# Edge-network messages summed as two float32r parts against a one-hot stationary operand

## The reference, cut to what matters

```python
def _L1_gnn_ref(x, edge_index, edge_attr, W1, b1, W2, b2, W3, b3, W4, b4):
    row, col = (edge_index[0], edge_index[1])
    h = jnp.concatenate([x[row], edge_attr], axis=1)
    h = jax.nn.relu(h @ W1 + b1)                 # [edges, 128]
    h = h @ W2 + b2
    agg = scatter_mean(h, col, x.shape[0])       # sum over a node's edges / their count
    g = jnp.concatenate([x, agg], axis=1)
    g = jax.nn.relu(g @ W3 + b3)
    return g @ W4 + b4
...
x = _layernorm(x + _L1_gnn_ref(x, edge_index, edge_attr_32, ...), axis=-1)
```

## Time and profile before

| | us |
|---|---|
| median of 3 runs | 1945.89 |
| lowest and highest run | 1943.58, 1948.28 |
| span of the profiled execution, first to last instruction | 1945.2 |
| mean granted TensorE clock, as a share of full speed | 0.815 |
| busy over the whole span: PE, DVE, ACT, POOL | 1270.0, 998.1, 739.7, 578.6 |
| busy share: PE, DVE, ACT, POOL | 65%, 51%, 38%, 30% |

### The profile page before, as it was taken

The page is one execution under the profiler, slowest core; times in us unless marked ns, Lnnn a source line. Parts: engine busy times, 40 slices in busy tenths (PEclk is TensorE's granted clock), DMA queues, the critical chain, the costliest instruction groups (busy, mean ns, idle before and its releaser), DMA issues.

```text
span 1945.2 us, 47461 instructions
## 1 busy us (share of the span) xinstructions
PE 1270.0 (65%) x19829; PEld 1164.5 (60%) x19830; DVE 998.1 (51%) x2349; ACT 739.7 (38%) x2012; POOL 578.6 (30%) x683
## 2 busy tenths in 40 slices
PE   5201001000002787778998999998799998998897
PEld 3200000000001666667897999998799998898897
DVE  8000002000010666674457566565788888887887
ACT  5000000000001777773213344343566666655464
POOL 2777777777772000000001444441010010000000
PEclk8555555555555999889997999998899999899999
DMA  7431000001010999997474888884766661344442
GB/s 222 141 133 35 15 15 13 14 27 38 13 54 35 357 370 379 387 369 265 174 289 175 315 308 304 301 306 170 252 247 233 224 247 56 143 168 158 175 178 92
DMA packets 86126, 359.64 MB, mean 185 GB/s; under 512 B 23740, under 2 KB 35281, under 8 KB 78929
## 3 DMA queue, kind: packets, MB, share of 16 engines
q1 hardware_dynamic: 72594, 348.83, 48.3%
q0 software_dynamic: 13312, 7.69, 1.7%
HBM read 250.77 MB, written 105.68 MB: 183 GB/s over the span
## 4 chain that ended last, share of the span: by engine, by line
PE 45%; another core or an unknown queue 21%; issue 12%; DVE 12%; ACT 7%; DMA 2%; SPq 1%; POOL 0%; ACTq 0%; DVEq 0%; POOLq 0%
PE ps L2998 8%; PE ps L3619 7%; PE ps L2650 7%; PE ps L2986 6%; PE ps L3266 5%; PE ps L3633 2%; DMA arena<-recs 2%; PE ps L2525 2%; PE ps L2510 1%; DVE arena L3208 1%; DVE arena L3209 1%; ACT arena L2570 1%; DVE arena L2389 1%; PE ps L3322 1%
## 5 line engine op out<-in xcount | busy, mean ns | idle before, releaser
L2178 POOL DMA_INDIRECT recs<-arena x416 | 423.8, 1019 | 164.9 <-issue 132.2
L3056 POOL CAST arena<-arena 128x512 f32<-128x512 bf16 (+1 forms) x175 | 119.4, 684 | 615.2 <-DMA arena<-hot_out 447.8
L3619 PE MATMUL ps<-arena 125*128 125x64 bf16 x5850 | 192.8, 194 | 10.0 <-issue 10.0
L3619 PEld LDWEIGHTS ps<-arena 125*128 125x128 bf16 x5850 | 187.7, 99 | 11.9 <-issue 11.8
L2998 PE MATMUL ps<-arena 128*128 128x125 f32 x1300 | 182.2, 282 | 0.0
L3665 ACT ACTIVATE arena<-ps,arena 128x64 f32<-128x64 f32 x650 | 141.0, 333 | 102.9 <-PE ps L3633 102.9
L2510 PE MATMUL ps<-arena 128*128 128x128 bf16 x625 | 66.9, 232 | 166.5 <-issue 157.3
L3142 DVE TENSOR_TENSOR arena<-ps,arena 128x512 f32<-128x512 f32 (+1 forms) x175 | 114.1, 653 | 118.4 <-PE ps L2986 115.4
L3089 ACT ACTIVATE arena<-arena 128x512 f32<-128x512 f32 (+1 forms) x175 | 105.0, 601 | 171.4 <-DVE arena L3142 171.4
L2570 ACT ACTIVATE arena<-ps 128x512 f32<-128x512 f32 (+1 forms) x192 | 83.8, 523 | 215.8 <-remote 183.7
L2998 PEld LDWEIGHTS ps<-arena 128*128 128x128 f32 x1300 | 158.8, 192 | 0.0
(11 more groups left out here) (385 smaller groups left out, 2414.5 us busy)
## 6 DMA issues: line engine op xcount, KB each, us to landing
arena<-ids_out SPq DMA_DIRECT2D x100, 832.0 KB, 6.2
arena<-hot_out SPq DMA_DIRECT2D x75, 832.0 KB, 6.2
arena<-e_out SPq DMA_DIRECT2D x25, 1664.0 KB, 6.9
arena<-adj_out SPq DMA_DIRECT2D x41, 800.0 KB, 6.5
e_out<-arena SPq DMA_DIRECT2D x25, 1024.0 KB
hot_out<-arena SPq DMA_DIRECT2D x25, 832.0 KB, 7.1
adj_out<-arena SPq DMA_DIRECT2D x25, 800.0 KB, 6.4
e_out<-arena SPq DMA_DIRECT2D x25, 640.0 KB
```

Of the source, the lines that this page charges most:

```text
L2178: nc.gpsimd.indirect_dma_start(out=recs, out_offset=bass.IndirectOffsetOnAxis(ap=slot_row[:, t:t + 1], axis=0), in_=rec_in[:, t, :], in_of ...
L3056: nc.gpsimd.tensor_copy(hot_e[s % NH][:, 0:len(js), :], hot_in[d % 2][:, js[0]:js[0] + len(js), :])\
L3619: ins = M(bank(step % 4, C, k * C), hot_r[d % 2][r][0:NP_, j * SLOTS:(j + 1) * SLOTS], px3[:, block_of(d, j), piece, r * C:(r + 1) * C], s ...
```

## The change

The scatter's operands change places, and its data become float32r, a 32-bit type with a shorter mantissa to which the writing engine rounds. A message is split in two parts, the rounded value and what rounding left off, and both are summed.

- ACT makes relu twice from the same `pre`: first into the first half of `act_two` (rounded to float32r), then into `whole` (float32).
- POOL subtracts the first part from `whole` and writes the second part, rounded again, into the second half of `act_two`. It does this for step s behind the cast of step s + 1. Its cast now writes float32r, into a ring `hot_e` of four instead of eight.
- PE scatters with the one-hot (128 slots x 128 columns) as stationary operand and both parts, 256 columns, as the moving one. A block's bank holds nodes on the partitions and 2 x 128 columns. It waits for POOL's subtraction (`act_rest`) too.
- After the block's last scatter DVE adds the two halves (`tensor_reduce` to `both`), PE transposes the 125x128 result into the same bank behind the 256 columns, one step later, and DVE multiplies by the reciprocals one step after that. `hid_step` and all that hangs on it stand two steps (`TURN_SUM`) later.
- `pre` is a ring of three instead of two; `whole` and `both` lie in `y1`. The memsets of `sel` move from step G7 - 1 to G7 + 4.
- What is float32r lies in a buffer of its own, `rounded`, at the place in `arena` where `act_out` and `hot_e` were.

```diff
+NE = 4
...
-        act_out = [e1_at([128, 4 * HID]) for _ in range(4)]
...
-        hot_e = [e1_at([128, 4, 128]) for _ in range(NH)]
+        act_two = [rounded[:, k * 8 * HID:(k + 1) * 8 * HID].rearrange("p (k t h) -> p k t h", t=2, h=HID)
+                   for k in range(4)]
+        hot_e = [rounded[:, (32 + 4 * k) * HID:(36 + 4 * k) * HID].rearrange("p (k n) -> p k n", n=128)
+                 for k in range(NE)]
...
+        pre.append(e2_at([128, 4 * HID]))
+        whole = [y1[:, (13 + 4 * k) * HID:(17 + 4 * k) * HID] for k in range(2)]
+        both = [y1[0:NP_, (11 + k) * HID:(12 + k) * HID] for k in range(2)]
...
+        TURN_SUM = 2
...
-            return 7 * (tiles(c)[-1] + 1) + LAG + 2
+            return 7 * (tiles(c)[-1] + 1) + LAG + TURN_SUM + 2
...
                     pe.wait_ge(sem("act_relued"), s + 1)
+                    pe.wait_ge(sem("act_rest"), s + 1)
                     for k, j in enumerate(groups(d)[g]):
-                        ins = M(bank(4 + d % 2, NP_), act_out[s % 4][:, k * HID:(k + 1) * HID],
-                                hot_e[s % NH][:, k, 0:NP_], start=j == 0, stop=j == NT, skip_group_check=True)
+                        ins = M(bank(4 + d % 2, 2 * HID), hot_e[s % NE][:, k, :],
+                                act_two[s % 4][:, k, :, :].rearrange("p t h -> p (t h)"), start=j == 0, stop=j == NT,
+                                skip_group_check=True)
                     ins.then_inc(sem("act_summed"), 1)
+                d, at = divmod(step - LAG - TURN_SUM, 7)
+                if at == 0 and 1 <= d <= NT:
+                    d -= 1
+                    pe.wait_ge(sem("both_added"), d + 1)
+                    nc.tensor.transpose(bank(4 + d % 2, NP_, 2 * HID), both[d % 2], ident[0:NP_, 0:NP_])\
+                        .then_inc(sem("sum_turned"), 1)
...
         def pool_edge2(pool):
+            def rest(s):
+                n = len(groups(s // 7)[s % 7])
+                pool.wait_ge(sem("act_relued"), s + 1)
+                nc.gpsimd.tensor_tensor(act_two[s % 4][:, 0:n, 1, :],
+                                        whole[s % 2][:, 0:n * HID].rearrange("p (k h) -> p k h", h=HID),
+                                        act_two[s % 4][:, 0:n, 0, :].bitcast(F32), ALU.subtract)\
+                    .then_inc(sem("act_rest"), 1)
...
-                if s >= NH:
-                    pool.wait_ge(sem("act_summed"), s - NH + 1)
-                nc.gpsimd.tensor_copy(hot_e[s % NH][:, 0:len(js), :], hot_in[d % 2][:, js[0]:js[0] + len(js), :])\
+                if s >= NE:
+                    pool.wait_ge(sem("act_summed"), s - NE + 1)
+                nc.gpsimd.tensor_copy(hot_e[s % NE][:, 0:len(js), :], hot_in[d % 2][:, js[0]:js[0] + len(js), :])\
                     .then_inc(sem("dst_hot"), 1)
+                if s >= 1:
+                    rest(s - 1)
+            rest(G7 - 1)
...
-                    A(act_out[step % 4][:, 0:m], pre[step % 2][:, 0:m], ACT.Relu).then_inc(sem("act_relued"), 1)
+                    A(act_two[step % 4][:, 0:m // HID, 0, :], pre[step % 3][:, 0:m].rearrange("p (k h) -> p k h", h=HID),
+                      ACT.Relu)
+                    if step >= 2:
+                        act.wait_ge(sem("act_rest"), step - 1)
+                    A(whole[step % 2][:, 0:m], pre[step % 3][:, 0:m], ACT.Relu).then_inc(sem("act_relued"), 1)
...
-                    if step >= 2:
-                        dve.wait_ge(sem("act_relued"), step - 1)
+                    if step >= 3:
+                        dve.wait_ge(sem("act_relued"), step - 2)
...
                     dve.wait_ge(sem("act_summed"), 7 * d + 7)
+                    if d >= 2:
+                        dve.wait_ge(sem("sum_turned"), d - 1)
+                    got = bank(4 + d % 2, 2 * HID)[0:NP_, :]
+                    V.tensor_reduce(both[d % 2], got.rearrange("p (t h) -> p h t", t=2), AX, ALU.add).then_inc(sem("both_added"), 1)
+                d, at = divmod(step - LAG - TURN_SUM - 1, 7)
+                if at == 0 and 1 <= d <= NT:
+                    d -= 1
+                    dve.wait_ge(sem("sum_turned"), d + 1)
```

More of the change, by code:

```diff
@@ L11 @@
 F16 = mybir.dt.float16
+F32R = mybir.dt.float32r
 U16 = mybir.dt.uint16
@@ L45 @@
 NH = 8
+NE = 4
+LOW_AT = 9464
+ROUNDED = 6144
 SLOTS = 128
@@ L212, in build @@
         ps = ctx.enter_context(nc.psum_tensor("ps", [128, 8 * BANK], F32))
-        arena = sb("arena", [128, ARENA])
         iota_i = sb("iota_i", [128, 128], I32)
@@ L222, in build @@
         flag = sb("flag", [1, 1], I32)
+        with nc.sbuf_tensor("arena", [128, ARENA], F32) as arena:
+            pass
+        sb("below", [128, LOW_AT])
+        rounded = sb("rounded", [128, ROUNDED], F32R)
         keep = Carver(arena)
@@ L278, in build @@
         px = e1_at([NP_, NT, PIECES, HID], BF16)
-        act_out = [e1_at([128, 4 * HID]) for _ in range(4)]
         hot_in = [e1_at([128, SB, 128], BF16) for _ in range(2)]
-        hot_e = [e1_at([128, 4, 128]) for _ in range(NH)]
+        assert e1_at.at == LOW_AT
+        act_two = [rounded[:, k * 8 * HID:(k + 1) * 8 * HID].rearrange("p (k t h) -> p k t h", t=2, h=HID)
+                   for k in range(4)]
+        hot_e = [rounded[:, (32 + 4 * k) * HID:(36 + 4 * k) * HID].rearrange("p (k n) -> p k n", n=128)
+                 for k in range(NE)]
+        e1_at.at += ROUNDED
         assert e1_at.at <= rest_at
@@ L2891, in hid_step @@
         def hid_step(c):
-            return 7 * (tiles(c)[-1] + 1) + LAG + 2
+            return 7 * (tiles(c)[-1] + 1) + LAG + TURN_SUM + 2
         OUT, EVICT, ROOT, SCALED, TURN, TURNED, HUP, HIGH, LEFT, MID, LOW = 3, 4, 9, 11, 13, 15, 17, 19, 21, 23, 25
-        E_STEPS = 7 * (NT + 1) + LAG + 2 + LOW + 1
+        E_STEPS = 7 * (NT + 1) + LAG + TURN_SUM + 2 + LOW + 1
         def started(step, off):
@@ L3139, in dve_edge2 @@
                     dve.wait_ge(sem("px_got"), step + 1)
-                    if step >= 2:
-                        dve.wait_ge(sem("act_relued"), step - 1)
-                    V.tensor_tensor(pre[step % 2][:, 0:m], bank(step % 4, m),
+                    if step >= 3:
+                        dve.wait_ge(sem("act_relued"), step - 2)
+                    V.tensor_tensor(pre[step % 3][:, 0:m], bank(step % 4, m),
                                     e1_in[d % 2][:, 4 * g * HID:4 * g * HID + m], ALU.add).then_inc(sem("e1_added"), 1)
@@ L3157, in dve_edge2 @@
                         dve.wait_ge(sem(f"rcp_in{c % 2}"), 16 * (c // 2 + 1))
-                    V.tensor_tensor(agg[:, d * NP_:(d + 1) * NP_], bank(4 + d % 2, NP_),
+                    V.tensor_tensor(agg[:, d * NP_:(d + 1) * NP_], bank(4 + d % 2, NP_, 2 * HID),
                                     rcp_row[c % 2][:, k * NP_:(k + 1) * NP_], ALU.mult).then_inc(sem("agg_read"), 1)
@@ L3161, in dve_edge2 @@
                     tables_att(dve, 0)
+                if step == G7 + 4:
+                    dve.wait_ge(sem("act_rest"), G7)
                     for k in range(2):
```

## The result

| | before | after |
|---|---|---|
| median of 4 runs, us | 1947.09 | 1995.86 |
| lowest and highest run | 1943.58, 1954.38 | 1993.27, 1996.91 |
| span of the profiled execution | 1945.2 | 1991.2 |
| first addition of the stage to end of the last scatter | 1060.05 to 1344.87: 284.8 | 1061.52 to 1387.72: 326.2 |

The change makes the kernel slower by 2.41%, ratio 1.0241 with a 95% interval of 1.0219 to 1.0263, some 48 us. Of the 46.0 us between the two profiled spans 41.4 lie in the edge stage, 1.7 in the tail behind the last scatter, 1.5 had come before the stage began, and the rest came after the tail.

The account below looks back on a forecast made before the run. POOL was to bound the edge stage: casts 100.6, subtractions 208.7 and shut-outs 29.3 make 338.6 us, ending the last scatter 56.1 us later; with about 2 us of tail, 2004.0 us, range 1962 to 2038.

Parts of the forecast that it names:

- Scatter tile at one pass: PE's scatter in the edge stage: a float32r tile of 256 columns takes 0.118 us, half of today's 0.235.
- the upper bound of 0.481: PE's scatter: float32r no faster than float32, 0.481 us a tile, 2115 us in all; chance 0.06.
- reading (a): POOL's subtraction priced from the small float32 row: 1.27 us for 512 elements, 0.73 for 256; chance 0.77 shared with (b).
- (b): POOL's subtraction priced from the row with one bfloat16 input: 1.05 and 0.62 us, total 1968 us.
- (c): POOL's subtraction on a line through both small rows: 0.78 and 0.51 us, total 1924; 0.12 with other faster ways.
- the dear one of 1.84: POOL's subtraction with a fixed cost of only 0.099 us: 1.84 us for 512 elements, total 2096 us; chance 0.05.
- ACT, DVE, the reduction: Edge stage loads hidden under the bound: ACT 224 us with two relus, DVE 175 us with 25 reductions of 0.42 us.
- The rings: Edge stage: four steps from subtraction to next subtraction take 4.8 us, 1.2 a step; ACT's two-step wait is not the slowest.
- The queue: POOL's edge-stage casts, 100.6 us, and subtractions, 208.7 us, run one after another with no gap added; with shut-outs 338.6 us.
- The shut-outs: Edge stage: DVE operations that keep POOL out cost it their length less 0.18 us each, together 29.3 us.
- The tail: Behind the last scatter: reduction, transpose, handovers, the later output matmul and two memsets add about 2 us.
- PE's clock: Edge stage rival: with PE busy about 62%, a lower clock at times adds 3 to 12 us; no chance of its own.

## Why the prediction was right, and where it was off

Forecast 2004.0 us, measured 1995.86, with POOL as the bound. By the steps of the text:

- *Scatter tile at one pass.* 0.118 us was taken. The weight loads are 0.117 us apart, as forecast, and the upper bound of 0.481 is out, but four tiles take 0.56 us until the next gather, 0.14 a tile: the last matmul of the row is followed by the gather only 0.56 - 3 x 0.117 = 0.21 us after its start. Over 650 tiles that is 14 us, and of the 71 us that PE was to save 58.9 came where PE was the bound. Here POOL's queue hid this. The Trainium skill (FP8 and Floating Point Precision, TensorE Precision Notes) gives four passes to true FP32, and the trace agrees: a float32 tile of 125 columns takes 0.235 us where a bf16 matmul of 128 takes 0.056, some four times as long. For reduced-precision FP32 it says that the number is truncated after the read, and gives no rate.
- *The subtraction, reading (a).* 1.27 us and 0.73 for the half were taken; the median is 1.273 and the two half groups in the timeline at 1076 and 1089 us take 0.74. Readings (b), (c) and the dear one of 1.84 are out. The step that carried the forecast was to take the fixed cost from the cast of the same engine, where two sizes were known, and only the slope from the small two-input row. The Trainium skill (GPSIMD Engine Reference, Elementwise — side-by-side cycle accounting) gives about 2.6 cycles an element at 1.2 GHz, and the measured slope, (1.273 - 0.74) / 256 = 0.0021 us or 2.5 cycles, agrees. The 1.26 us that the prediction drew from that page does not follow from it alone: its two figures make 1.11 + 0.06 = 1.17 us by an estimate, a tenth of a microsecond below the measurement.
- *ACT, DVE, the reduction.* A relu to float32r takes 0.625 us and the second 0.627; the reduction 0.414 us for the 0.42 taken. That none of it costs time while POOL is the bound was argued in the prediction; in the run without the subtraction all of it is there and the stage takes 100 us less.
- *The rings.* The ring of four steps at 1.2 us a step and ACT's wait for the subtraction of two steps before were taken to cost nothing. For the wait the run with three buffers bears it out; the ring of four was not tried by itself.
- *The queue, the term of the sum that was mis-sized.* A full step was taken as 0.613 + 1.27 = 1.88 us of POOL. It is 1.785 us: the cast's record begins 0.05 us before the subtraction's ends, and the same at the other side. Over 150 full steps that is 14 us, which is the difference in the stage: 341 us from the first addition to the last scatter were forecast (1401.0 - 1060.05), 326.2 measured. The total came nearer (8 us) than the stage (15 us) by luck: 3 us arose outside stage and tail, and the median lies 4.7 us above the profiled span, whose run was the fastest of four, where the forecast had 0.7. I had looked at the gaps between POOL's records for a cost above zero and had not asked whether they could be negative. Seven casts in the earlier trace rows had an allowance left over, which hid it.
- *The shut-outs.* 29 us were taken. After 150 x 1.785 us and 25 half steps of about (0.355 + 0.68) us, POOL's 323 us from 1063.5 to its end leave 29 us, 6 of them waits for ACT. So the shut-outs came out at some 23 us, 6 less than taken, and waits for ACT, which the prediction had put at nothing, made up for it: the step is near, its exact fit is chance.
- *The tail.* +2 us forecast. From the end of the last scatter to the gathers of the attention layer it was 9.8 us (1344.87 to 1354.69) and is 11.5 (1387.72 to 1399.27), +1.7.
- *PE's clock.* 0.96 in the stage with PE at 78% of its time where about 62% had been forecast, between the two levels in the mean; no row shows that the stage waited for it.
- *What the prediction said too simply.* That an operation of DVE waits for the one instruction in progress on POOL. It often does: the layer-norm operation L929 took 1.12 us at 1199.18, and the cast behind the running subtraction was held up in its turn. But five of the 25 comparisons, of 2.08 to 2.19 us, sat through two instructions of POOL, and now and then it is far more, as this part of the timeline after shows, where the casts and subtractions went on while DVE's operation of 0.46 us lasted 5.29:

```profile
1376.80 5.29 DVE L3237 TENSOR_TENSOR arena<-arena 125x296 bf16<-125x296 f32 x1
...
1381.35 0.41 POOL L3087 CAST rounded<-arena 128x256 fp32r<-128x256 bf16 x1
...
1384.07 2.85 POOL L3075 TENSOR_TENSOR rounded<-y,rounded 128x512 fp32r<-128x512 f32 x2 [2.31 <-ACT y L3127]
```

In the changed kernel this is rare (this one, and one comparison of 5.65 us); in the kernel with the cut subtraction it moved the comparison's mean to 2.78 us. All 16 waits of this length in the edge stages of this case's traces (2 here, 9 with the cut subtraction, 4 with three buffers, 1 with casts on ScalarE; operations of 4.2 to 6.2 us) end alike: counted back from the operation's end, its own time begins 0.1 to 0.2 us before the end of the last instruction that POOL had to give, and then POOL stands idle for 2.3 to 2.75 us, since the relu that it needs hangs on the addition behind that operation. Here the operation's own 0.46 us begin at 1381.63, POOL's half cast ends at 1381.76, and POOL is idle until 1384.07.

## What to carry to other kernels

Before work is taken off the engine that orders a stage, add up the queue of every engine that receives some, with the rate that this engine has for this kind of operation: some 59 us that TensorE could save were worth nothing against a subtraction that takes 1.27 us on GpSimd and 0.70 on VectorE. Take the fixed cost of an unmeasured size from the same engine's operations of two sizes, and look also for records that overlap. And two engines that shut each other out are no two places for work: counting busy time alone promised 1918 us for shared-out work, and it gave 1947.

## What the runs showed of the hardware

- Four float32r tiles against 128x128 weights take 0.56 us from the start of the scatter to the next gather with 256 moving columns and 0.48 us with 128, four float32 tiles of 128 columns 0.95 us (the swapped float32 kernel). A tile is 0.14, 0.12 and 0.24 us. The float32r weight loads inside a row are 0.117 and 0.113 us apart.
- GpSimd's two-input subtraction of 128x512 float32 takes 1.273 us and its successor starts 0.05 us before its record ends; its cast to float32r costs the 0.612 us that the cast to float32 did.
- VectorE's operations with two SBUF inputs, its wide comparison and even its 125x4 TENSOR_SCALAR (0.763 us in the mean of the stage, 0.17 alone) wait for GpSimd. Its addition of one input from PSUM and one from SBUF does not: 0.685 us in the mean of 150 beside the subtraction on GpSimd, 0.681 with it moved to VectorE. Behind GpSimd instructions that follow each other without a gap a wait can outlast several of them: 5.29 us for an operation of 0.46, 4.78 us for one of 1.08. All 16 waits of this length in the edge stages ended only as GpSimd's row of instructions did. Why others get through after one or two instructions was not found.
